# Second chunk of a fused attention and feed-forward kernel: V's copies and low halves ahead of a row tile and a row of outputs

## The chip, the cores and the metric

The kernel runs on one core of one Trainium2 chip. The metric is the device time of one execution in microseconds (us). The engines are called as in the profile: PE is TensorE, DVE is VectorE, ACT is ScalarE, POOL is GpSimd, SP is SyncE, which here only issues DMAs. Each engine runs its own queue of instructions in order and waits on semaphores that the others raise.

## What is computed

The input is 4096 rows of 512 numbers (2 x 2048 x 512). Each row goes through a latent attention block and a feed-forward block with ternary weights, each behind a layer norm and with a layer norm on its result before the residual is added. Cut to what matters:

```
h  = layernorm(x)
Q, V = h @ Wq.T + bq, h @ Wv.T + bv             # 16 heads of 32
logits = Q . latent_keys / sqrt(32)             # 64 latents per head
w, idx = top_k(logits, 4);  p = softmax(w)
attn = (sum_k p_k * latent[idx_k] + V) @ Wo.T + bo
x  = x + layernorm(attn)
g  = layernorm(x)
u, gt = g @ ternary(W_up).T, g @ ternary(W_gate).T   # 2048 wide
x  = x + layernorm((silu(u) * gt) @ ternary(W_down).T)
```

Every matrix product works on float16 pairs: a float32 operand is split in a high half (a copy to float16) and a low half (what the copy left over), and both are multiplied.

## The kernel before

The rows are cut into eight chunks of 512, each of four row tiles of 128. The code of one chunk is a `body(i, kind, att, ffn, nxt)` that every engine has for itself: `"first"`, `"second"`, then a loop of `"mid"` bodies, `"last"` and `"tail"`. A body of chunk i holds the attention of chunk i, the feed-forward of chunk i-1, and the first layer norm of chunk i+1, interleaved. The order on each engine is the order of the calls in its body. `late` is true in the second body alone; there the ternary weights are still being made.

At the end of the second body stands the seam that the change touches. The row of work on each engine is:

- **PE** (from the call `v(0)` on): V of two banks (`v(0)`, `v(1)`), the down products of row tiles 0 and 1 (`down`, L692), `v(2)`, `v(3)` (L539), the weighted latents added to V's accumulators (`weigh`, L631), `down(2)`, then the output projection `wo(0)` to `wo(3)` (L651, 12 matmuls each), and `down(3)`. `wo(0)` waits before each of its four groups k for the low half `a_lo` number k+1. The next body begins with Q (`q`, L539 with wq), which needs the next chunk's four transposed row tiles (XT), and with `upgate(0, half)` and `upgate(1, half)` (L673), of which half 0 needs the first two transposed tiles of X1T and half 1 the last two.
- **ACT**: `f_rows(t)` (L980) scales row tile t of the down product into the output buffer; `s1_rows(1, t)` normalises row tile t of the next chunk (L787, tile xn) and makes its high half (L800, tile halves); `vw(m)` copies V's accumulator m out of its bank (L943, tile p32, shown as p) and makes its high half (L948, qaT_hi). xn is one buffer, so `s1_rows` of tile t waits for the low half of tile t-1. p32 has two buffers, so `vw(2)` and `vw(3)` wait for the low halves 0 and 1. The high half of row tile 2 waits until the transpose of tile 0 has read its buffer.
- **POOL**: `s1_lo(1, t)` makes the row tile's low half (L1233), `f_out(t)` adds the residual to the output buffer (L1221) and releases the store, `low_a(m)` makes the low halves of V (L1186, qaT_lo), `rstd_f` and `rstd_y` compute reciprocal deviations (L1146).
- **DVE**: `f_a(t)`, `f_b(t)` make statistics and factors of a down row (rcf L1554, nbf L1560), `y_a(t)` takes an output projection out of its bank (L1599) with its statistics, `y_b`, `y_c` make the residual sum and the second layer norm's factors (x L1619, nbx L1633), `t2_lo` its low half (L1472), `f_row(3)` the last output row (L1588). `f_b(2)` stands ahead of `y_a(1)`.
- **SP**: store 0, reload 0, store 1, reload 1 of the residual (L431, L440; both of t wait for `f_out(t)`), then the four transposes XT (L371), then reload 2 and store 2, then the four transposes X1T (L371).

Of the kernel before, what the change touches and what calls it, by code (L numbers as in the profile page):

```python
# [80 lines left out]
def build(nc, x, Wq, Wv, Wo, small, bo, Wu, Wg, Wd, out):  # L81
    NCH = x.shape[0] * x.shape[1] // CH
    with ExitStack() as ctx:
# [148 lines left out]
        def wait(eng, s, c, per, n):  # L232


            v = c * per + max(n, 0)
            if not isinstance(v, int) or v > 0:
                eng.wait_ge(s, v)


        def wait_p(eng, c, tiles):  # L240

            for s in range(2):
                wait(eng, p_t[s], c, 32, 16 * ((tiles + 1 - s) // 2))
# [52 lines left out]
        def residual(is_last):  # L296

            return x_in if is_last else x1

        def split_buffers(kind, c, t):  # L300


            if kind == "first" and c == 0:
                return (qaT[t // 2][:, :, :].rearrange("p k t -> p (k t)").bitcast(F32)[:, (t % 2) * D:(t % 2 + 1) * D],
                        PT[:, 0, 2 * t:2 * t + 2, :].rearrange("p k t -> p (k t)"))
            if kind == "first":
                return Lb[:, t % 2, 0:D // NL, 0:NL], out_buf[t % 2].bitcast(F16)
            return xn[:, :], halves[:, t % 2, :]
# [7 lines left out]
        def wide(v, rows):  # L316

            return v.rearrange("p (a l) -> p a l", l=NL) if len(rows.shape) == 3 else v
# [13 lines left out]
        def down_bank(kind, t):  # L332

            if kind == "last" and t >= 2:
                return ring[:, plans["last"][("WO", 0, t - 2)][0], :]
            return ug[:, t, :]
# [429 lines left out]
        def _(act):  # L766
            def body(i, kind, att, ffn, nxt):
# [3 lines left out]
                def s1_rows(c, t):  # L771

                    wait(act, ln1_bias, i + c, 1, 1)

                    if kind == "first" and c == 0:
                        pass
                    elif kind == "first" and t < 2:

                        wait(act, p_ready, i, TT, 3 + t)
                    elif kind == "first":  # L780
                        wait(act, x_lo, i + c, TT, t - 1)
                    elif t:
                        wait(act, x_lo, i + c, TT, t)
                    else:
                        wait(act, x1_lo, i - 1, TT, TT)
                    rows, half = split_buffers(kind, c, t)
                    act.activation(rows, wide(x_in[:, t, :], rows), ACT.Identity, scale=rs1[:, t:t + 1],  # L787
                                   bias=nb1[:, t:t + 1]).then_inc(xn1_ready, 1)
                    wait(act, xn1_ready, i + c, TT, t + 1)

                    if kind == "first" and c == 0:
                        pass
                    elif kind == "first" and t < 2:

                        wait(act, p_raw, i, TT, TT)
                    elif t < 2:
                        wait_p(act, i + c, 0)
                    else:
                        wait(act, x_t[t % 2], i + c - 1, 32, 16)
                    act.activation(wide(half[:, 0:D], rows), rows, ACT.Copy).then_inc(x_hi, 1)  # L800
# [136 lines left out]
                def vw(m):  # L937
                    wait(act, vw_done, i, KD, m + 1)
                    if m < 2:
                        wait(act, q_lo, i, KD, KD)  # L940
                    else:
                        wait(act, a_lo, i, KD, m - 1)
                    act.activation(p32[:, m % 2, :], ring[:, plan[("VW", 0, m)][0], :], ACT.Identity,  # L943
                                   scale=PROJ, bias=bvs[:, m:m + 1]).then_inc(a32_ready, 1)
                    wait(act, a32_ready, i, KD, m + 1)

                    wait(act, l_done, i, 8, 8)
                    act.activation(qaT[0][:, m, :], p32[:, m % 2, :], ACT.Copy).then_inc(a_hi, 1)  # L948
# [26 lines left out]
                def f_rows(t):  # L975

                    wait(act, f_bias, j, TT, t + 1)

                    wait(act, out_stored[(t + 2) % 4], j, 16, 16 if t >= 2 else 0)
                    act.activation(out_buf[t % 2], down_bank(kind, t), ACT.Identity, scale=rcf[:, t % 2:t % 2 + 1],  # L980
                                   bias=nbf[:, t % 2:t % 2 + 1]).then_inc(f_sum, 1)
# [83 lines left out]
                late = kind == "second"  # L1065
# [42 lines left out]
                    f_rows(0)  # L1108
                if nxt:
                    s1_rows(1, 0)  # L1110
                    s1_rows(1, 1)
                    f_rows(1)
                if att:
                    for m in range(KD):
                        vw(m)
                if nxt:
                    s1_rows(1, 2)
                    s1_rows(1, 3)
                    f_rows(2)
                elif att:  # L1120
                    f_rows(1)
# [6 lines left out]
                if kind == "last":  # L1128
                    f_rows(2)
                    f_rows(3)  # L1130

            bodies(act, body)


        @block.gpsimd
        def _(pool):
# [19 lines left out]
            def body(i, kind, att, ffn, nxt):  # L1156
# [27 lines left out]
                def low_a(m):  # L1184
                    wait(pool, a_hi, i, KD, m + 1)
                    pool.tensor_tensor(qaT[1][:, m, :], p32[:, m % 2, :], qaT[0][:, m, :], ALU.subtract).then_inc(a_lo, 1)  # L1186
# [31 lines left out]
                def f_out(t):  # L1218

                    wait(pool, f_sum, j, TT, t + 1)  # L1220
                    pool.tensor_tensor(out_buf[t % 2], out_buf[t % 2], residual(kind == "tail")[:, t, :],  # L1221
                                       ALU.add).then_inc(out_ready, 1)
# [7 lines left out]
                def s1_lo(c, t):  # L1230
                    wait(pool, x_hi, i + c, TT, t + 1)
                    rows, half = split_buffers(kind, c, t)
                    pool.tensor_tensor(wide(half[:, D:2 * D], rows), rows, wide(half[:, 0:D], rows), ALU.subtract).then_inc(x_lo, 1)  # L1233

                def rstd_f(t):
                    rstd(rsf[:, t % 2:t % 2 + 1], vaf[:, t % 2:t % 2 + 1], 1, f_var, j, TT, t + 1, f_rstd)
# [43 lines left out]
                late = kind == "second"  # L1280
# [30 lines left out]
                if nxt:  # L1311
                    rstd_f(1)
                    s1_lo(1, 0)
                    s1_lo(1, 1)
                    f_out(1)
                if att:
                    for m in range(KD):
                        low_a(m)
                if nxt:
                    s1_lo(1, 2)  # L1320
                    s1_lo(1, 3)
                    rstd_f(2)
                elif ffn:
                    rstd_f(1)
                    f_out(1)
# [19 lines left out]
                elif ffn:  # L1345
                    f_out(3)

            bodies(pool, body)


# [511 lines left out]
```

## Time and profile before

| what | us |
|---|---|
| median of 3 runs | 1040.43 (1039.85 to 1041.40) |
| the profiled execution, its device time | 1039.87 |
| its span in the trace | 1038.0 |
| PE busy | 967.7 (93%) |
| DVE, POOL, ACT busy | 733.5, 542.9, 514.2 |

The mean granted TensorE clock of the profiled execution is 0.979 of full speed. The profiled execution has 1.9 us outside its span. The second body's seam lies between 186 and 246 us of the span; the first waits for transposed tiles of the chunk after it end at 245 us, and from there on PE shows no wait for another engine until 330 us. Times below are us from the start of the span.

### The profile page before, as it was taken

The numbers are of one execution on the slowest core, as the hardware profiler recorded it, in microseconds if no ns is written. First come the engines' busy times: TensorE is split into PE (matmuls) and PEld (weight loads), VectorE is DVE, ScalarE is ACT, GpSimd is POOL, SyncE is SP. The second block draws the span as 40 slices with busy tenths as digits, with TensorE's granted clock in tenths as the row PEclk, the third lists the DMA queues.
The fourth block names the chain that finished last, engine by engine and source line by source line (L and its number), as shares of the span: only waits on it lengthen the run. The fifth ranks groups of instructions, "written<-read, shape, count | busy, mean of one in ns | idle before, by whom it ended". The sixth has DMA issues, their size and how long they took to land.

```text
span 1038.0 us, 17906 instructions
## 1 busy us (share of the span) xinstructions
PE 967.7 (93%) x5738; PEld 470.3 (45%) x5738; DVE 733.5 (71%) x2664; ACT 514.2 (50%) x803; POOL 542.9 (52%) x452
## 2 busy tenths in 40 slices
PE   3374999999999999999999999999999999999997
PEld 2331544345444454445444454445444454445443
DVE  7986899556993779845994768936896669845433
ACT  4867886345444455245444445344553454423430
POOL 2476356654665546564565445654465546643330
PEclk9786999999999999999999999999999999999999
DMA  8935503433123311233023331244022321212001
GB/s 261 399 97 90 164 1 82 100 88 98 22 31 93 84 58 31 53 99 92 11 39 84 77 82 21 41 103 110 10 41 61 91 42 21 41 41 62 1 1 41
DMA packets 149330, 76.91 MB, mean 74 GB/s; under 512 B 135824, under 2 KB 135824, under 8 KB 148112
## 3 DMA queue, kind: packets, MB, share of 16 engines
q1 hardware_dynamic: 149264, 76.18, 29.3%
q8 instruction: 23, 0.38, 0.2%
q14 instruction: 43, 0.35, 0.1%
HBM read 34.21 MB, written 8.39 MB: 41 GB/s over the span
## 4 chain that ended last, share of the span: by engine, by line
PE 60%; DVE 17%; ACT 7%; issue 6%; POOL 6%; DMA 4%; SPq 0%; DVEq 0%; ACTq 0%; POOLq 0%
PE ug L673 34%; PE ug L692 12%; PE ring L539 8%; PE ring L651 4%; DVE Lr L1514 2%; PE ring L587 2%; POOL halves L1233 1%; DVE halves L1472 1%; DVE ugt L1477 1%; DVE v L1492 1%; DMA X1T<-halves 1%; DVE stx L1622 1%; DVE row L1599 1%; DVE x L1619 1%; DVE sty L1602 1%
## 5 line engine op out<-in xcount | busy, mean ns | idle before, releaser
L1210 POOL TENSOR_TENSOR hT<-ugt,hT 128x512 f16<-128x512 f32 x128 | 166.9, 1304 | 164.6 <-ACT hT L973 164.6
L673 PE MATMUL ug<-X1T,TU 128*128 128x512 f16 (+1 forms) x1152 | 245.1, 356 | 6.4 <-DVE ugt L1482 4.6
L673 PE MATMUL ug<-X1T,TG 128*128 128x512 f16 (+1 forms) x1152 | 244.9, 355 | 0.0
L692 PE MATMUL ug<-TD,hT 128*128 128x512 f16 x960 | 212.7, 381 | 2.4 <-ACT TD L854 2.4
L960 ACT ACTIVATE ugt<-ug,cu 128x512 f32<-128x512 f32 x128 | 87.9, 687 | 202.8 <-PE ug L673 202.0
L673 PEld LDWEIGHTS ug<-X1T,TU 128*128 128x128 f16 x1152 | 109.9, 98 | 116.8 <-DVE ugt L1482 5.6
L673 PEld LDWEIGHTS ug<-X1T,TG 128*128 128x128 f16 x1152 | 112.7, 98 | 108.7
L1477 DVE SCALAR_TENSOR_TENSOR ugt<-ugt,ug 128x512 f32<-128x512 f32 x128 | 87.2, 681 | 99.2 <-ACT ugt L960 98.0
L692 PEld LDWEIGHTS ug<-TD,hT 128*128 128x128 f16 x960 | 93.6, 98 | 118.8 <-issue 5.3
L1514 DVE MATCH_REPLACE8 Lr<-v,Lb 128x68 f32<-128x68 f32 x512 | 102.3, 211 | 0.0
L1541 DVE BATCH_NORM_STATS2 stf<-ug 128x6 f32<-128x512 f32 x30 | 20.8, 694 | 99.4 <-PE ug L692 99.4
L1482 DVE SCALAR_TENSOR_TENSOR ugt<-ugt,ug 128x512 f32<-128x512 f32 x128 | 87.9, 687 | 4.4
L539 PE MATMUL ring<-XT,wq_hi 128*128 128x512 f16 (+1 forms) x288 | 79.2, 362 | 7.6 <-DVE wq_lo L1450 5.8
L1192 POOL TENSOR_TENSOR Lb<-Lb,v 128x1024 f32<-128x1024 f32 x32 | 63.2, 1976 | 37.9 <-DVE Lr L1514 37.9
L973 ACT ACTIVATE hT<-ugt 128x512 f16<-128x512 f32 x128 | 79.6, 622 | 3.1 <-DVE ugt L1482 3.1
L1492 DVE MAX8 v<-Lb 128x8 f32<-128x64 f32 x512 | 69.0, 208 | 0.4
L539 PE MATMUL ring<-XT,wv_hi 128*128 128x512 f16 x224 | 66.6, 379 | 0.0
L1204 POOL TENSOR_TENSOR p<-Lb,r 128x1024 f32<-128x1024 f32 x24 | 45.6, 1900 | 34.8 <-DVE Lb L1529 34.8
L651 PE MATMUL ring<-wo_hi,qaT_hi 128*128 128x512 f16 x128 | 50.4, 394 | 2.9 <-POOL qaT_lo L1177 2.0
L935 ACT ACTIVATE halves<-p 128x1024 f16<-128x1024 f32 x29 | 30.4, 1048 | 45.7 <-POOL p L1204 41.2
L539 PE MATMUL ring<-XT,wq_lo 128*128 128x512 f16 (+1 forms) x144 | 52.1, 362 | 0.0
L814 ACT ACTIVATE xn<-x,nbx,rsx 128x512 f32<-128x512 f32 x28 | 22.7, 810 | 57.4 <-DVE nbx L1633 38.5
(195 smaller groups left out, 1479.2 us busy)
## 6 DMA issues: line engine op xcount, KB each, us to landing
out_dram<-Lr SPq DMA_DIRECT2D x32, 256.0 KB, 3.2
x_in<-in_x SPq DMA_DIRECT2D x7, 1024.0 KB, 5.5
x<-in_x SPq DMA_DIRECT2D x28, 256.0 KB, 3.3
PT<-in_Wd SPq DMA_DIRECT2D x8, 512.0 KB, 6.9
hT<-in_Wu SPq DMA_DIRECT2D x4, 512.0 KB, 9.4
hT<-in_Wg SPq DMA_DIRECT2D x4, 512.0 KB, 15.0
x_in<-in_Wd SPq DMA_DIRECT2D x4, 512.0 KB, 4.8
x_in<-in_x SPq DMA_DIRECT2D x4, 256.0 KB, 4.5
```

The lines of the kernel that those rows point to most:

```text
L539: last = pe.matmul(bank[:, cols], wT[w][a][:, k, m * P:(m + 1) * P], XT[:, b, k, cols], start=(n == 1), stop=(stop and n == 3 * KD), skip_ ...
L651: last = pe.matmul(ring[:, bank, :], qaT[a][:, k, t * P:(t + 1) * P], wT[2][b][:, k, :], start=(n == 1), stop=(n == 3 * KD))
L673: last = pe.matmul(ug[:, 2 * (e % 2) + s, cols], w[:, k, e * P:(e + 1) * P], X1T[:, b, k, cols], start=(k == 0 and b == 0), stop=(k == KD ...
L692: last = pe.matmul(down_bank(kind, t), hT[:, a, e, t * P:(t + 1) * P], td[:, e, :], start=(first and e == of[0] and a == 0), stop=(final a ...
L960: act.activation(ugt[:, e % 2, :], ug[:, 2 * (e % 2), :], ACT.Tanh, scale=cu[:, 0:1]).then_inc(tanh_ready, 1)
L973: act.activation(hT[:, 0, e, :], ugt[:, 2 + e % 2, :], ACT.Copy).then_inc(h_hi, 1)
L1192: pool.tensor_tensor(buf, buf, v8[:, t % 2, :, 0:1].broadcast_to([P, H, NL]), ALU.subtract).then_inc(shifted, 1)
L1210: pool.tensor_tensor(hT[:, 1, e, :], ugt[:, 2 + e % 2, :], hT[:, 0, e, :], ALU.subtract).then_inc(h_lo, 1)
L1477: dve.scalar_tensor_tensor(out=ugt[:, e % 2, :], in0=ugt[:, e % 2, :], scalar=1.0, in1=ug[:, 2 * (e % 2), :], op0=ALU.add, op1=ALU.mult).t ...
L1482: dve.scalar_tensor_tensor(out=ugt[:, 2 + e % 2, :], in0=ugt[:, e % 2, :], scalar=HS, in1=ug[:, 2 * (e % 2) + 1, :], op0=ALU.mult, op1=ALU ...
L1492: last = dve.max(v8[:, t % 2, h, :], Lb[:, t % 2, h, 0:NL])
L1514: last = dve.match_replace(Lr[:, h, :], v8[:, t % 2, h, :], Lb[:, t % 2, h, :], HIT)
```

## The change

In the second body alone, two calls on ACT and two on POOL go behind four others. On ACT, `s1_rows(1, 1)` and `f_rows(1)` stood ahead of the four `vw`; now the four `vw` come first, then `f_rows(1)`, then `s1_rows(1, 1)`. On POOL, `s1_lo(1, 1)` and `f_out(1)` stood ahead of the four `low_a`; now the four `low_a` come first, then `f_out(1)`, then `s1_lo(1, 1)`. No instruction is added or taken away, and the orders on PE, DVE and SP are the same.

```
@@ ACT @@
                     f_rows(0)
                 if nxt:
                     s1_rows(1, 0)
-                    s1_rows(1, 1)
-                    f_rows(1)
+                    if not late:
+                        s1_rows(1, 1)
+                        f_rows(1)
                 if att:
                     for m in range(KD):
                         vw(m)
                 if nxt:
+                    if late:
+                        f_rows(1)
+                        s1_rows(1, 1)
                     s1_rows(1, 2)
@@ POOL @@
                 if nxt:
                     rstd_f(1)
                     s1_lo(1, 0)
-                    s1_lo(1, 1)
-                    f_out(1)
+                    if not late:
+                        s1_lo(1, 1)
+                        f_out(1)
                 if att:
                     for m in range(KD):
                         low_a(m)
                 if nxt:
+                    if late:
+                        f_out(1)
+                        s1_lo(1, 1)
                     s1_lo(1, 2)
```

POOL's queue at the end of the second body, before, from `f_out(0)` on (x4 and x2 are instructions in a row that read alike; the brackets name the semaphores waited for, f_sum comes from `f_rows`, x_hi from `s1_rows`, a_hi from `vw`):

```order
69 L1221 TENSOR_TENSOR Lr<-Lr,x1 128x512 [waits f_sum]
70 L1146 TENSOR_TENSOR rsf<-vaf,nh 128x1 [waits f_var]
71 L1233 TENSOR_TENSOR halves<-xn,halves 128x512 [waits x_hi] x2
72 L1221 TENSOR_TENSOR Lr<-Lr,x1 128x512 [waits f_sum]
73 L1186 TENSOR_TENSOR qaT_lo<-p32,qaT_hi 128x512 [waits a_hi] x4
74 L1233 TENSOR_TENSOR halves<-xn,halves 128x512 [waits x_hi] x2
75 L1146 TENSOR_TENSOR rsf<-vaf,nh 128x1 [waits f_var]
76 L1146 TENSOR_TENSOR rsy<-vay,nh 128x1 [waits y_var]
```

The same place of POOL's queue after the change (line numbers are four higher there):

```order
69 L1225 TENSOR_TENSOR Lr<-Lr,x1 128x512 [waits f_sum]
70 L1150 TENSOR_TENSOR rsf<-vaf,nh 128x1 [waits f_var]
71 L1237 TENSOR_TENSOR halves<-xn,halves 128x512 [waits x_hi]
72 L1190 TENSOR_TENSOR qaT_lo<-p32,qaT_hi 128x512 [waits a_hi] x4
73 L1225 TENSOR_TENSOR Lr<-Lr,x1 128x512 [waits f_sum]
74 L1237 TENSOR_TENSOR halves<-xn,halves 128x512 [waits x_hi] x3
75 L1150 TENSOR_TENSOR rsf<-vaf,nh 128x1 [waits f_var]
76 L1150 TENSOR_TENSOR rsy<-vay,nh 128x1 [waits y_var]
```

The four low halves moved ahead of `f_out(1)` and of one row tile; the three row tiles that are left now stand in one piece.

ACT's queue at the same place, before, from `s1_rows(1, 0)` on (vw_done comes from PE's `weigh`, a_lo and x_lo from POOL):

```order
191 L787 ACTIVATE xn<-x_in,nb1,rs1 128x512 [waits x1_lo,ln1_bias]
192 L800 ACTIVATE halves<-xn 128x512 [waits p_t1,p_t0,xn1_ready]
193 L787 ACTIVATE xn<-x_in,nb1,rs1 128x512 [waits x_lo,ln1_bias]
194 L800 ACTIVATE halves<-xn 128x512 [waits p_t1,p_t0,xn1_ready]
195 L980 ACTIVATE Lr<-ug,nbf,rcf 128x512 [waits f_bias]
196 L943 ACTIVATE p32<-ring,bvs 128x512 [waits q_lo,vw_done]
197 L948 ACTIVATE qaT_hi<-p32 128x512 [waits l_done,a32_ready]
```

And after the change:

```order
192 L800 ACTIVATE halves<-xn 128x512 [waits p_t1,p_t0,xn1_ready]
193 L943 ACTIVATE p32<-ring,bvs 128x512 [waits q_lo,vw_done]
194 L948 ACTIVATE qaT_hi<-p32 128x512 [waits l_done,a32_ready]
...
199 L943 ACTIVATE p32<-ring,bvs 128x512 [waits a_lo,vw_done]
200 L948 ACTIVATE qaT_hi<-p32 128x512 [waits l_done,a32_ready]
201 L980 ACTIVATE Lr<-ug,nbf,rcf 128x512 [waits f_bias]
202 L787 ACTIVATE xn<-x_in,nb1,rs1 128x512 [waits x_lo,ln1_bias]
```

The eight instructions of `vw` moved ahead of three: the two of row tile 1 and the row of the second down product.

## Rows read from the trace of the kernel before

**Rows 1.** The chain that ended last: shares of the span by engine.

```profile
PE 60%; DVE 17%; ACT 7%; issue 6%; POOL 6%; DMA 4%; SPq 0%; DVEq 0%; ACTq 0%; POOLq 0%
```

**Rows 2.** Timeline of PE: start, length (us), instruction, idle before and its releaser.

```profile
189.83 9.63 PE L692 MATMUL ug<-TD,hT 128*128 128x512 f16 x36 [1.86 <-ACT TD L854]
...
204.56 0.63 PE L631 MATMUL ring<-PT,latV_hi 64*32 64x512 f16 x16
...
212.91 0.38 PE L651 MATMUL ring<-wo_hi,qaT_hi 128*128 128x512 f16 x1
...
215.69 0.39 PE L651 MATMUL ring<-wo_hi,qaT_hi 128*128 128x512 f16 x1 [0.42 <-POOL qaT_lo L1186]
...
224.12 7.07 PE L692 MATMUL ug<-TD,hT 128*128 128x512 f16 x32
231.03 0.59 PE L539 MATMUL ring<-XT,wq_hi 128*128 128x512 f16 x2
...
243.13 1.04 PE L673 MATMUL ug<-X1T,TU 128*128 128x256 f16 x8
...
245.35 1.03 PE L673 MATMUL ug<-X1T,TU 128*128 128x256 f16 x8 [0.30 <-DMA X1T<-halves]
```

**Rows 3.** Timeline of ACT, same columns.

```profile
204.05 0.63 ACT L800 ACTIVATE halves<-xn 128x512 f16<-128x512 f32 x1
206.66 0.81 ACT L787 ACTIVATE xn<-x_in,nb,rs 128x512 f32<-128x512 f32 x1 [1.99 <-POOL halves L1233]
...
208.71 0.68 ACT L943 ACTIVATE p<-ring,bvs 128x512 f32<-128x512 f32 x1
...
215.49 0.63 ACT L800 ACTIVATE halves<-xn 128x512 f16<-128x512 f32 x1 [0.38 <-DMA XT<-halves]
217.45 0.81 ACT L787 ACTIVATE xn<-x_in,nb,rs 128x512 f32<-128x512 f32 x1 [1.33 <-POOL halves L1233]
```

**Rows 4.** Timeline of POOL.

```profile
205.13 1.16 POOL L1233 TENSOR_TENSOR halves<-xn,halves 128x512 f16<-128x512 f32 x1
...
209.33 1.27 POOL L1221 TENSOR_TENSOR Lr<-Lr,x 128x512 f32<-128x512 f32 x1
...
213.24 2.39 POOL L1186 TENSOR_TENSOR qaT_lo<-p,qaT_hi 128x512 f16<-128x512 f32 x2 [0.40 <-ACT qaT_hi L948]
...
219.00 1.16 POOL L1233 TENSOR_TENSOR halves<-xn,halves 128x512 f16<-128x512 f32 x1 [1.65 <-ACT halves L800]
220.12 0.55 POOL L1146 TENSOR_TENSOR rsf<-vaf,nh 128x1 f32<-128x1 f32 x1
```

**Rows 5.** Timeline of DVE.

```profile
220.70 0.16 DVE L1554 TENSOR_TENSOR rcf<-rsf,cf 128x1 f32<-128x1 f32 x1 [2.15 <-POOL rsf L1146]
...
221.03 0.74 DVE L1599 SCALAR_TENSOR_TENSOR row<-ring,clo,bo_b 128x512 f32<-128x512 f32 x1
...
239.58 0.74 DVE L1588 SCALAR_TENSOR_TENSOR Lr<-ug,rcf,x_kept 128x512 f32<-128x512 f32 x1
```

**Rows 6.** The chain in order of time, cut to two transposes: start, length, what.

```profile
211.65 3.76 DMA XT<-halves
...
242.16 3.05 DMA X1T<-halves
```

**Rows 7.** Timeline of the last chunk: weigh on PE, V's copies on ACT, low halves on POOL.

```profile
917.01 0.62 PE L631 MATMUL ring<-PT,latV_hi 64*32 64x512 f16 x16
...
917.92 0.69 ACT L943 ACTIVATE p<-ring,bvs 128x512 f32<-128x512 f32 x1 [6.25 <-PE ring L631]
...
922.02 2.40 POOL L1186 TENSOR_TENSOR qaT_lo<-p,qaT_hi 128x512 f16<-128x512 f32 x2 [0.28 <-ACT qaT_hi L948]
```

**Rows 8.** PE by stretches: us, PE busy (instructions), granted clock, DMA share, GB/s.

```profile
101.00:102.00 1.00, 0.00 (x0) 1.00 0.27 53
...
190.00:191.00 1.00, 1.00 (x3) 0.50 0.58 66
```

**Rows 9.** Timeline of PE in the first body, before the second chunk's Q.

```profile
102.15 0.59 PE L539 MATMUL ring<-XT,wq_hi 128*128 128x512 f16 x2 [1.67 <-DMA XT<-Lr]
```

More of the change, by code:

```diff
@@ L1110, in body @@
                     s1_rows(1, 0)
-                    s1_rows(1, 1)
-                    f_rows(1)
+                    if not late:
+                        s1_rows(1, 1)
+                        f_rows(1)
                 if att:
@@ L1116, in body @@
                 if nxt:
+                    if late:
+                        f_rows(1)
+                        s1_rows(1, 1)
                     s1_rows(1, 2)
@@ L1313, in body @@
                     s1_lo(1, 0)
-                    s1_lo(1, 1)
-                    f_out(1)
+                    if not late:
+                        s1_lo(1, 1)
+                        f_out(1)
                 if att:
@@ L1319, in body @@
                 if nxt:
+                    if late:
+                        f_out(1)
+                        s1_lo(1, 1)
                     s1_lo(1, 2)
```

## The prediction, written before the changed kernel was run

> **What bounds the kernel now.** I read first the chain that ended last. PE holds 60% of it and DVE 17% [rows 1], so PE sets the end in most places and something else in a few, and the question is what sets it at this seam. PE's timeline shows three waits there. Before the third group of `down` PE waits 1.86 us for the ternary weights [rows 2]; the change comes later than that. In `wo(0)` it waits for the low halves of V, the row that starts at 215.69 [rows 2]. And at 245.35 the first matmul of `upgate(0, 1)` waits for the last transpose X1T [rows 2, 6].
>
> The third wait is the important one. From 245.35 on PE runs without waiting, so whatever moves that instant moves the end. What moves it is not PE's own pace but a second path, which the timelines give step by step: `f_out(1)` on POOL, 209.33 to 210.60 [rows 4]; store 1 and reload 1 on SP; the transpose XT of tile 0 from 211.65, landed 3.76 later at 215.41 [rows 6]; the high half of tile 2 on ACT, which waits for that landing [rows 3]; its low half on POOL; tile 3 on ACT at 217.45, which waits for POOL [rows 3]; its low half on POOL from 219.00 and behind it `rstd_f(2)` at 220.12 [rows 4]; `f_b(2)` on DVE at 220.70, which had waited 2.15 us for it, and behind it `y_a(1)` at 221.03 [rows 5]. From there DVE is busy with `y_a`, `y_b`, `y_c` and `t2_lo` in a row, down to the transpose X1T from 242.16, landed 3.05 later at 245.21 [rows 6].
>
> **What the change takes away: the wait in `wo(0)`.** The 48 matmuls of `wo` take from 212.91 to 224.12, 11.21 us. At the pace of `down(3)`, 32 in 231.03 - 224.12 = 6.91 us or 0.216 each [rows 2], they would take 10.37. So 0.84 us is lost, all of it ahead of groups 3 and 4 of `wo(0)`. When will the low halves be ready after the change? The last chunk shows the same instructions with nothing ahead of them: `vw(0)` starts 917.92 - 917.01 = 0.91 us after `weigh(0)`, and the fourth low half ends at 922.02 + 2.40 = 924.42, which is 6.50 us after `vw(0)` starts [rows 7]. Here `weigh(0)` starts at 204.56 [rows 2], so `vw(0)` starts at 205.47; ACT is free from 204.68 on [rows 3] and POOL from 206.29 [rows 4], before the first low half could start anyway. The fourth low half ends at 205.47 + 6.50 = 211.97 instead of 213.24 + 2.39 = 215.63 [rows 4]. PE reaches `wo(0)` at 212.91, so the wait goes entirely: **-0.84 us for PE**, if nothing else bound it.
>
> **What it delays: `f_out(1)`, and with it the second path.** On POOL `f_out(1)` now stands behind the four low halves, so it starts at 211.97 instead of 209.33: 2.64 later, say 2.6, since neighbours on POOL overlap by 0.04. (On ACT, `f_rows(1)` comes behind `vw(3)` and ends half a us before that; it does not decide.) SP issues its DMAs in order and has `f_out(1)` in front of all four transposes, so transpose 0 goes from 211.65 to 214.25. The rest of the path follows step by step with nothing to absorb it. Row tile 1 costs nothing of its own: its low half follows `f_out(1)` on POOL and ends at 214.4, and transpose 1 is not due before 213.07 + 2.6. ACT's tile 2 waits for transpose 0's landing, now at 218.0, tile 3 for POOL behind that, `rstd_f(2)` for tile 3's low half, DVE for `rstd_f(2)`. DVE has waited 2.15 us there already and will wait longer; `y_a(1)` starts at 223.6. Between it and the last X1T DVE has no idle stretch over 0.5 us, so I take no slack out of it. The last X1T lands at 247.8 and PE starts `upgate(0, 1)` at 245.35 + 2.6 = 247.95. That `wo` is done 0.84 earlier is worth nothing, since it only makes PE wait longer. **+2.6 us on the path that sets the end.**
>
> The bounds of this term. If the clock had not been low from 190 on (below), `weigh(0)` would start up to 1.7 us earlier, but POOL is only free at 206.29 [rows 4] and needs twice 2.40 us for the four low halves [rows 7] plus a gap of 0.1 to 0.3 between them; `f_out(1)` would start at about 211.2, +1.9. So the term lies between 1.9 and 2.6. What else is delayed has room: the last XT lands near 226.5, and Q wants it at 231.03 - 0.84 = 230.2 [rows 2]. The second X1T lands at about 240.0, half a us before `upgate(0, 0)` wants it. `f_row(3)` ends at 240.32 + 2.6 = 242.9 [rows 5], and `upgate(1, 0)` waits for it from 243.13 - 0.84 = 242.3 on [rows 2]: 0.6 us that vanishes in the longer wait behind it.
>
> **What PE's longer idle costs.** `upgate(1, 0)` takes two steps of 0.87, from 243.0 to 244.8, and then PE has nothing to do until 247.95: 3.1 us, after 0.6 us just before. In the trace of before, an idle time of 1.86 us ending at 189.83 [rows 2], with one of 0.5 us shortly ahead of it, is followed by the granted clock at 0.50, the lower level of 1.2 GHz [rows 8]. It cost 1.7 us: 36 matmuls took 9.63, where at full clock they take 36 x 0.216 + 0.16 = 7.94 [rows 2]. Against that, an idle time of 1.67 us ending at 102.15 [rows 9] left the clock at 1.00 [rows 8]. The new idle time is nearly twice the longer of the two, so I take the fall as the likelier: **+1.7 us**. PE is the bound from there on, so all of it counts. The bounds are 0 and 3.4 (a fall that lasts twice as long). [...]
>
> **The sum.** -0.84 is hidden; 2.6 + 1.7 = +4.3 us. On the profiled execution of before that is 1039.87 + 4.3 = 1044.2, on the median 1040.43 + 4.3 = 1044.7. Not every execution need have the full term at both places, so I forecast between the two: **1044.4 us**, range of this case alone 1043.4 to 1045.2.
>
> **The rivals.**
>
> (B) The clock stays at full speed after the idle time. For it: the row that did not fall after 1.67 us [rows 8, 9]. Against it: 3.1 us is well above both rows. Then only the path counts: +1.9 to +2.6, so 1042.3 to 1043.0.
>
> (C) The second path has slack that I do not see, and the gain in `wo(0)` stays: not slower, but faster. One mechanism would do it: SP's transposes would have to be waiting for something other than `f_out(1)`, such as PE's last read of XT by `v(3)`, and DVE likewise at `f_b(2)`. It decides if the transposes start less than 0.4 us later than before. The time would be 1040.43 - 0.84 + (0 to 0.3) = 1039.6 to 1039.9. Against it: store 1 starts within 0.05 us of `f_out(1)`'s end and the transpose follows the two DMAs at once, and `v(3)` is over by 204.56 [rows 2]. I give it little.
>
> (D) The clock falls and stays low twice as long, because Q's successor begins with short matmuls and an interrupted stretch. +2.6 + 3.4 = +6.0, so 1046.4.
>
> (E) The change has its waits elsewhere, and absorbs part of the delay on DVE: `y_a(0)` comes 0.84 earlier. But DVE idles between `y_a(0)` and `f_b(2)`, so this moves nothing; what is left is a delay of about 1 us without a fall of the clock, 1041.0 to 1041.8.
>
> **How the numbers follow.** Forecast 56%, B 28%, C 4%, D 6%, E 6%. The range goes from 1042.0, which takes in B whole, to 1046.0, which leaves out most of D, C and E: 1042.0 to 1046.0 holds about 84% by this count, and I keep it, as the terms are known to no better than some tenths. A measurement of this kernel can tell about 0.2% or 2.1 us from no change, that is 1038.3 to 1042.5. Slower by more: the forecast, D, and some three quarters of B, 0.83. Within: the low part of B, E and C, 0.15. Faster by more than 0.2% has no mechanism here, since the wait removed is 0.84: 0.02.
>
> **What the profile of the changed kernel would show.** Right: no wait in `wo(0)`, whose 48 matmuls take 10.4 us; `vw(0)` at about 205.5; `f_out(1)` at 212.0; the first XT issued at 214.2; `rstd_f(2)` at 222.7; `y_a(1)` at 223.6; a PE wait for X1T of about 3 us ending near 247.9; and a granted clock of 0.5 just before or after that. Wrong: an X1T that lands before 246.5 (the path has slack), or a wait for X1T of 3 us with the clock at 1.00 throughout, which is B. A time below 1041 would mean that the second path is not what sets the end.

## The result, and the profile after

The changed kernel takes 1044.76 us, the median of 6 runs from 1043.57 to 1045.15. The kernel before, with six runs by now, takes 1040.15 (1039.59 to 1041.40). The ratio is 1.0039, with a 95% interval of 1.0028 to 1.0049, which is 2.9 to 5.1 us; by the medians it is 4.6 us slower. The forecast was 1044.4 with a range of 1042.0 to 1046.0. The profiled execution of after has a span of 1043.1 us against 1038.0.

This is PE's timeline of the changed kernel over the same stretch; the rows answer to [rows 2]:

```profile
190.25 9.60 PE L692 MATMUL ug<-TD,hT 128*128 128x512 f16 x36 [1.86 <-ACT TD L854]
...
204.96 0.63 PE L631 MATMUL ring<-PT,latV_hi 64*32 64x512 f16 x16
...
213.30 0.38 PE L651 MATMUL ring<-wo_hi,qaT_hi 128*128 128x512 f16 x1
...
223.66 7.07 PE L692 MATMUL ug<-TD,hT 128*128 128x512 f16 x32
...
243.83 1.05 PE L673 MATMUL ug<-X1T,TU 128*128 128x256 f16 x8 [0.80 <-DVE Lr L1596]
...
248.79 1.87 PE L673 MATMUL ug<-X1T,TU 128*128 128x256 f16 x8 [3.04 <-DMA X1T<-halves]
```

The 48 matmuls of `wo` now take 223.66 - 213.30 = 10.36 us, where they took 11.21: the 0.84 us that the change was good for have been taken. In their place stand a new wait of 0.80 us for `f_row(3)`, and one of 3.04 us for the last X1T, which was 0.30 before. To compare the two traces, take off what this execution was already late before the seam: the third group of down matmuls starts at 190.25 against 189.83, 0.42 us.

POOL and ACT of the changed kernel (they answer to [rows 3, 4]):

```profile
207.29 2.40 POOL L1190 TENSOR_TENSOR qaT_lo<-p,qaT_hi 128x512 f16<-128x512 f32 x2 [0.59 <-ACT qaT_hi L948]
209.97 2.40 POOL L1190 TENSOR_TENSOR qaT_lo<-p,qaT_hi 128x512 f16<-128x512 f32 x2 [0.28 <-ACT qaT_hi L948]
212.32 1.27 POOL L1225 TENSOR_TENSOR Lr<-Lr,x 128x512 f32<-128x512 f32 x1
213.55 1.16 POOL L1237 TENSOR_TENSOR halves<-xn,halves 128x512 f16<-128x512 f32 x1
219.63 1.16 POOL L1237 TENSOR_TENSOR halves<-xn,halves 128x512 f16<-128x512 f32 x1 [4.93 <-ACT halves L800]
222.43 1.15 POOL L1237 TENSOR_TENSOR halves<-xn,halves 128x512 f16<-128x512 f32 x1 [1.65 <-ACT halves L800]
223.54 0.55 POOL L1150 TENSOR_TENSOR rsf<-vaf,nh 128x1 f32<-128x1 f32 x1
```

```profile
205.87 0.69 ACT L943 ACTIVATE p<-ring,bvs 128x512 f32<-128x512 f32 x1 [0.78 <-PE ring L631]
...
218.93 0.63 ACT L800 ACTIVATE halves<-xn 128x512 f16<-128x512 f32 x1 [3.31 <-DMA XT<-halves]
```

DVE, and the chain in order of time, of the changed kernel (they answer to [rows 5, 6]). DVE waits 6.03 us for `rstd_f(2)` where it waited 2.15:

```profile
224.13 0.16 DVE L1562 TENSOR_TENSOR rcf<-rsf,cf 128x1 f32<-128x1 f32 x1 [6.03 <-POOL rsf L1150]
...
224.46 0.74 DVE L1607 SCALAR_TENSOR_TENSOR row<-ring,clo,bo_b 128x512 f32<-128x512 f32 x1
```

```profile
214.63 4.21 DMA XT<-halves
...
245.60 3.05 DMA X1T<-halves
248.79 5.04 PE ug L673 x32
```

The chain contains the whole second path: V's copies and low halves, `f_out(1)`, the transpose XT, the two row tiles, DVE's row of work (with a last piece on ACT), the transpose X1T. Its last row above shows the price of the clock: the 32 matmuls of `upgate(0, 1)` and `upgate(1, 1)` take 5.04 us, where before the same chain has them at 3.65. The granted clock (stretch, PE busy, clock, DMA share, GB/s) says why. It is at 0.50, the level of 1.2 GHz, from a little before PE resumes:

```profile
247.00:248.00 1.00, 0.00 (x0) 1.00 1.12 210
248.00:249.00 1.00, 0.21 (x2) 0.63 1.31 342
249.00:250.00 1.00, 1.00 (x6) 0.50 0.55 147
250.00:251.00 1.00, 1.00 (x7) 0.50 0.97 295
251.00:252.00 1.00, 1.00 (x8) 0.67 1.04 442
252.00:253.00 1.00, 1.00 (x11) 1.00 0.24 98
```

So the 5.1 us between the two spans are 0.42 us of lateness before the seam, 2.57 us by which `f_out(1)` starts later (212.32 - 0.42 - 209.33), 0.45 us by which the first XT takes longer to land (4.21 against 3.76), 1.39 us of the lower clock, and 0.3 us behind the seam, most of it in one later wait for X1T (0.70 us at 488.8, where it was 0.46).

### The profile page after: what moved, and what is told of

Its sections match the earlier page's. It is cut to its first block, busy times and chain, and to the rows that moved or that the text cites. A ratio compares the mean times of both kernels' runs of the same rounds, so it can differ in the third digit from the quotient of the medians.

```text
span 1043.1 us, 17906 instructions
## 1 busy us (share of the span) xinstructions
PE 968.3 (93%) x5738; PEld 471.0 (45%) x5738; DVE 733.8 (70%) x2664; ACT 514.1 (49%) x803; POOL 543.6 (52%) x452
## 4 chain that ended last, share of the span: by engine, by line
PE 61%; DVE 16%; ACT 7%; issue 6%; POOL 6%; DMA 3%; SPq 0%; DVEq 0%; ACTq 0%; POOLq 0%
PE ug L673 34%; PE ug L692 13%; PE ring L539 8%; PE ring L651 4%; DVE Lr L1522 2%; PE ring L587 2%; DVE ugt L1485 1%; POOL halves L1237 1%; POOL qaT_lo L1190 1%; DVE v L1500 1%; DMA X1T<-halves 1%; DVE stx L1630 1%; DVE halves L1480 1%; DVE x L1627 1%; DVE row L1607 1%
```

## Experiments

Each was timed beside the kernel before on the same chip (one chip for the first eight, another for the last two), and each ratio is taken against those runs. The kernel before had a median of 1039.73 (23 runs) beside the first four, 1040.48 (27 runs) beside the next four and 1040.53 (23 runs) beside the last two.

The traces of these kernels can also be compared over the seam alone, whatever came before or after it: from the start of the third group of down matmuls to the start of the first matmul of 512 columns of `upgate(2)`. The kernel before takes 60.55 us for it and the changed kernel 64.96. These are single executions.

**Which half of the change costs?** The change moves two things behind V's copies: row tile 1, and the second down row with `f_out(1)`. One kernel moves the row tile alone. Cut from ACT, and the same on POOL with `s1_lo` and `f_out`:

```
                     s1_rows(1, 0)
-                    s1_rows(1, 1)
+                    if not late:
+                        s1_rows(1, 1)
                     f_rows(1)
                 if att:
                     for m in range(KD):
                         vw(m)
                 if nxt:
+                    if late:
+                        s1_rows(1, 1)
```

> Half of the change: row tile 1 (on ACT and POOL) goes behind V's copies and low halves, the second down row stays ahead of them. Theory (the store row f_out(1) holds back SP's transposes, and the path through them sets the end): f_out(1) ends at about 209, transpose 0 goes at once, transpose 1 at about 215 and tile 3's low half ends where it did before. The wait in wo(0) is gone but hidden. Time 1040.2, between 1039.7 and 1041.0. Rival (row tile 1's own lateness is what costs, since tiles 2 and 3 queue behind it): the time stays near the changed kernel's, 1043.5 to 1045.

Measured: 1040.23 (12 runs), ratio 1.0005 (0.9996 to 1.0015). The theory holds. POOL's timeline of this kernel, whose seam begins 1.18 us later than that of before (third down group at 191.01):

```profile
208.57 1.27 POOL L1224 TENSOR_TENSOR Lr<-Lr,x 128x512 f32<-128x512 f32 x1 [1.16 <-ACT Lr L980]
209.81 2.39 POOL L1189 TENSOR_TENSOR qaT_lo<-p,qaT_hi 128x512 f16<-128x512 f32 x2
212.49 2.40 POOL L1189 TENSOR_TENSOR qaT_lo<-p,qaT_hi 128x512 f16<-128x512 f32 x2 [0.28 <-ACT qaT_hi L948]
215.09 1.16 POOL L1236 TENSOR_TENSOR halves<-xn,halves 128x512 f16<-128x512 f32 x1 [0.21 <-ACT halves L800]
...
220.69 1.15 POOL L1236 TENSOR_TENSOR halves<-xn,halves 128x512 f16<-128x512 f32 x1 [1.65 <-ACT halves L800]
```

Row tile 1's low half starts at 215.09, 5.7 us later than in the kernel before by its own start, and yet tile 3's starts at 220.69, 0.5 us later than before once the 1.18 is off. A row tile behind V's copies costs next to nothing, because in the kernel before the tiles behind it had been waiting for the transpose anyway. One part of the expectation was missed: PE still waits in `wo(0)`. In this execution the clock stayed up behind 190 (more on that below), so PE reached `wo(0)` sooner.

```profile
214.94 0.39 PE L651 MATMUL ring<-wo_hi,qaT_hi 128*128 128x512 f16 x1 [0.42 <-POOL qaT_lo L1189]
```

The other kernel moves the down row alone and leaves the row tile ahead:

```
                     s1_rows(1, 0)
-                    s1_rows(1, 1)
-                    f_rows(1)
+                    s1_rows(1, 1)
+                    if not late:
+                        f_rows(1)
                 if att:
                     for m in range(KD):
                         vw(m)
                 if nxt:
+                    if late:
+                        f_rows(1)
```

> The other half: the second down row goes behind V's copies and low halves, row tile 1 stays ahead. Theory: the copies start 2.7 us later than in the changed kernel, f_out(1) and the transposes with them, so the last X1T and the end come 2.7 us later than there: 1047.4, between 1046.5 and 1048.5. Rival (row tile 1's lateness costs): it is on time here, so 1040 to 1041.

Measured: 1046.34 (5 runs from 1045.91 to 1046.60), ratio 1.0062 (1.0049 to 1.0075). This is the half that costs, and by itself it costs more than the whole change. It is 1.6 us above the changed kernel rather than 2.7, just below the expected range. I had counted the copies as starting 2.7 us later. `f_out(1)` starts at 214.30, 2.0 us later than in the changed kernel (2.3 with both starts of the seam counted), and the first XT lands 3.80 us after its issue instead of 4.21, so the last X1T is used 1.8 us later than in the changed kernel. PE now waits three times, and the clock falls twice:

```profile
242.67 1.04 PE L673 MATMUL ug<-X1T,TU 128*128 128x256 f16 x8 [2.41 <-DMA X1T<-halves]
...
245.39 1.89 PE L673 MATMUL ug<-X1T,TU 128*128 128x256 f16 x8 [0.24 <-DVE Lr L1594]
...
250.34 1.55 PE L673 MATMUL ug<-X1T,TU 128*128 128x256 f16 x8 [2.12 <-DMA X1T<-halves]
```

```profile
244.00:245.00 1.00, 1.00 (x6) 0.50 0.00 0
...
248.00:249.00 1.00, 0.22 (x2) 1.00 0.68 135
...
251.00:252.00 1.00, 1.00 (x7) 0.50 0.83 262
```

The first of these falls does not add its whole price: PE was going to wait for X1T again at 250.

**Is it the order on SP?** The changed kernel, with the first transpose taken out from behind `f_out(1)`:

```
                     for t in range(2):
                         out(t)
                         if nxt:
                             reload(t)
+                        if kind == "second" and t == 0:
+                            s1(0)
                 if nxt:
-                    for t in range(TT):
+                    for t in range(1 if kind == "second" else 0, TT):
                         s1(t)
```

> The changed kernel, with one more move on SP in the second body: the transpose of row tile 0 ahead of store 1 and reload 1, so that it no longer waits for f_out(1). Theory: the high half of tile 2 no longer waits for its landing, tile 3's low half ends 2.7 us earlier than in the changed kernel, the time falls back to 1040.5 (1040.0 to 1041.2; up to 1.4 more if an idle time of some 1.6 us still lowers the clock). Rival (POOL's three row tiles in one piece are the cause, whatever SP does): 1043.5 to 1045.

Measured: 1040.51 (11 runs), ratio 1.0002 (0.9993 to 1.0012). With one DMA moved, the changed kernel is back at the time of the kernel before. SP's timeline shows the transpose going 6 us before store 1:

```profile
205.56 0.65 SPq L440 DMA_DIRECT2D x<-in_x  x1
206.86 1.23 SPq L371 DMA_TRANSPOSE XT<-halves  x1
212.98 0.34 SPq L431 DMA_DIRECT2D out_dram<-Lr  x1
```

`f_out(1)` itself is nearly as late here as in the changed kernel. It starts 21.42 us after the third down group, where the kernel before has 19.50 and the changed kernel 22.07 (the clock stayed up behind 190 here too, so V's copies came sooner; the 1.92 us are the prediction's lower bound of 1.9 for this case). The last X1T is used 55.57 us after the third down group, against 55.52 before and 58.54 in the changed kernel. What costs is therefore not that the output row comes late, but that SP keeps the first transpose behind it. PE's timeline has a surprise:

```profile
245.84 1.03 PE L675 MATMUL ug<-X1T,TU 128*128 128x256 f16 x8 [2.89 <-DMA X1T<-halves]
```

PE waited 2.89 us, and the clock was at 1.00 all the same in every microsecond from 243 to 252. PE waited that long because it came early, with no wait in `wo(0)` and the full clock behind 190:

```profile
245.00:246.00 1.00, 0.16 (x2) 1.00 1.05 318
246.00:247.00 1.00, 1.00 (x11) 1.00 0.58 131
```

I come back to this below.

**Does DVE pass the delay on?** The changed kernel, with `y_a(1)` put into the time in which DVE waits for `rstd_f(2)`:

```
                 if att:
                     y_a(0)
+                    if late:
+                        y_a(1)
                 if nxt:
                     f_b(2)
                 if att:
-                    y_a(1)
+                    if not late:
+                        y_a(1)
                     y_b(0)
```

> The changed kernel, with one more move on DVE in the second body: y_a(1) ahead of f_b(2), so that DVE uses the time in which it waits for rstd_f(2). Theory (DVE's row of work behind f_b(2) passes every delay on to the last X1T): the last X1T lands 1.9 us earlier than in the changed kernel; 1042.9 if the clock still falls, 1041.5 if the shorter idle time of 2.0 us leaves it up. Rival (DVE is not on the path): 1044 to 1045, as the changed kernel.

Measured: 1043.01 (5 runs from 1042.42 to 1044.93), ratio 1.0038 (1.0025 to 1.0051). The median is the one expected with the fall of the clock, and the clock does fall in its profile (0.50 from 248 to 250). But the interval overlaps with that of the changed kernel, so this run alone does not tell the theory from its rival. The trace says more: X1T is used at 246.79, with the third down group at 189.49, so 57.30 us after it, where in the changed kernel it is 58.54. The move saves 1.2 us of the path, not 1.9. That DVE passes the delay on is shown by this trace and not by the times.

**Both moves, with and without the change.**

> The changed kernel with both moves, transpose 0 ahead of store 1 on SP and y_a(1) ahead of f_b(2) on DVE, in the second body. Theory: the last X1T lands before PE wants it, so the 0.84 us that the change takes out of wo(0) and the 0.47 us that PE waited for X1T before it both count: 1.3 under the kernel before, 1038.9 (1038.3 to 1039.6). Rival (something else sets the end at this seam): 1040 or more.

> The kernel before, with the same two moves on SP and DVE and without the change. Theory: only the 0.47 us wait for X1T goes, the wait in wo(0) stays: 1039.7 (1039.2 to 1040.3), 0.8 above the kernel with the change and both moves. Rival (the moves on SP and DVE alone bring the whole gain): the same time as that kernel.

Measured: 1039.57 with the change (11 runs), ratio 0.9991 (0.9982 to 1.0000); 1040.07 without it (11 runs), ratio 0.9996 (0.9987 to 1.0005). The signs and the order are the expected ones. With the second path shortened the change is no longer a loss, and the medians differ by 0.5 us of the 0.8 forecast; but the two intervals overlap, so that the saved wait in `wo(0)` now counts is likely and not shown by these times. The two traces show a part of it: the seam takes 59.59 us with the change and 59.91 without, 0.3 us apart. With the change X1T still comes too late for PE, which waits 0.20 us for it:

```profile
245.38 1.03 PE L675 MATMUL ug<-X1T,TU 128*128 128x256 f16 x8 [0.20 <-DMA X1T<-halves]
```

**What does the lower clock cost?** To take the idle time away without the wait, the first pass of the middle loop was written out, and 12 spare matmuls were put where PE waits. The loop alone first, as control:

```
+            body(2, "mid", True, True, True)
-            with eng.Fori(2, NCH - 1) as i:
+            with eng.Fori(3, NCH - 1) as i:
```

> Control: the changed kernel with the first pass of the loop over the middle chunks written out ahead of the loop, the same work in the same order. Expected 1044.7 (1044.0 to 1045.4), as the changed kernel, with the clock at 0.50 after the wait for X1T.

Measured: 1045.00 (5 runs), ratio 1.0048 (1.0034 to 1.0061). It behaves like the changed kernel: X1T waited for 3.04 us, clock at 0.50 behind it. Then, in that pass, ahead of `upgate(0, 1)`:

```
                 for half in range(2):
+                    if kind == "mid" and isinstance(i, int) and half == 1:
+                        wait(pe, q32_ready, i, KD, 1)
+                        for n in range(12):
+                            pe.matmul(ring[:, plan["Q", 0, 0][0], :], wT[0][0][:, 0, 0:P], XT[:, 0, 0, :],
+                                      start=True, stop=True)
                     upgate(0, half)
```

> The control with 12 spare matmuls of 512 columns into a free bank (their result is not used), 2.6 us of PE work where PE waits for the last X1T. Theory (about 1.4 us of the loss is the lower clock after that idle time): the clock stays at 1.00 through the first products of the third chunk, X1T lands as late as in the control, and the time is 1.4 us under the control, 1043.3 (1042.7 to 1043.8). Rival (the clock costs nothing there): the control's time or more.

Measured: 1042.29 (11 runs), ratio 1.0013 (1.0004 to 1.0022). More work for PE makes the kernel faster by 2.7 us, and the ranges do not overlap (1040.75 to 1042.99 against 1044.51 to 1046.62). That is below the expected range of 1042.7 to 1043.8: 1.4 us were expected. In the two traces the seam itself gives the expected part of that. Control first, then filled:

```profile
249.17 1.87 PE L674 MATMUL ug<-X1T,TU 128*128 128x256 f16 x8 [3.04 <-DMA X1T<-halves]
...
255.63 1.90 PE L674 MATMUL ug<-X1T,TU 128*128 128x512 f16 x8
```

```profile
248.40 1.03 PE L674 MATMUL ug<-X1T,TU 128*128 128x256 f16 x8 [0.45 <-DMA X1T<-halves]
...
253.43 1.90 PE L674 MATMUL ug<-X1T,TU 128*128 128x512 f16 x8
```

From the landing of X1T to the first full matmul of `upgate(2)` the control takes 6.46 us and the filled kernel 5.03: 1.43 us, at clocks of 0.50 and 1.00. X1T is used 58.6 and 58.5 us after the third down group, so the path is as long in both. That the lower clock costs 1.4 us here is shown. The other 1.3 us of the difference between the medians are not explained by it. In the profiled pair, PE's waits for X1T at the later seams come to 2.3 us in the control and 0.6 in the filled kernel; whether the spare matmuls have any part in that stays open, since nothing behind the seam differs. All that follows the seam takes between 786.4 and 788.4 us in the twelve traces of this document, so two single executions can differ by as much without a cause in the kernel.

**Can the waits for X1T at the later seams be had, and the free half of the change with them?** Before, PE waits 1.5 us for X1T behind the seam in three places. One kernel has the move on DVE in the second and all middle bodies and nothing else (`if nxt:` where the piece above has `if late:`); the other adds the half of the change that costs nothing.

> The kernel before (no change), with one move on DVE in the second and in every middle body: y_a(1) ahead of f_b(2). Theory: the path through DVE is a little late at the later seams too (PE waits 1.5 us for X1T there in all, 0.3 us at the second body's seam), so those waits go: 1.8 under the kernel before, and the wait in wo(0) stays. Rival (the waits for X1T are run to run noise of the transposes and would stay): no difference.

Measured: 1039.74 (11 runs), ratio 0.9997 (0.9988 to 1.0005). No difference that can be told, so the expectation of 1.8 us missed. The waits say what went wrong: at the second body's seam PE no longer waits for X1T, and the seam is 0.4 us shorter (60.19). Of the later waits, two of 0.5 and one of 0.6 us in the kernel before, one of 0.5 and the one of 0.6 are still there. The one of 0.6 is at the seam before the tail, where the move does not apply; I had not looked where the three were.

> The same move on DVE in the second and in every middle body, with the half of the change that costs nothing: in the second body row tile 1 behind V's copies and low halves, the second down row ahead of them. Theory: the wait in wo(0) goes as well and now counts, since nothing else is late: 0.8 under the kernel with the move on DVE alone, 2.6 under the kernel before. Rival (the wait in wo(0) is hidden by another one): the same as with the move on DVE alone.

Measured: 1039.23 (12 runs), ratio 0.9990 (0.9982 to 0.9999). This is the lowest median of all, 1.3 us under the kernel before where 2.6 were forecast. Its interval just leaves out 1, as one of ten intervals, and overlaps with that of the DVE move alone, 0.5 us above it. So it is probably better than the kernel before, by a tenth of a percent, and half of what I forecast. The trace shows that "nothing else is late" did not hold. The seam takes 59.86 us, 0.3 less than with the DVE move alone; the clock stayed up behind 190, PE still waits 0.40 us in `wo(0)`, and then again for X1T:

```profile
245.66 1.03 PE L673 MATMUL ug<-X1T,TU 128*128 128x256 f16 x8 [1.58 <-DMA X1T<-halves]
```

## Why the prediction was right

The forecast was slower by 4.3 us, made of +2.6 for the second path, +1.7 for the clock and 0.84 that hides. Measured is 4.6. Step by step, with the 0.42 us by which this execution came late to the seam added to the forecast times:

- `vw(0)` at 205.89 forecast, 205.87 measured. The copies and low halves of the last chunk [rows 7] were the right measure for this seam.
- `f_out(1)` at 212.39, measured 212.32. The first XT issued at 214.67, measured 214.63.
- `y_a(1)` at 224.0, measured 224.46; the last X1T used at 248.37, measured 248.79. Both are 0.4 to 0.5 late, and all of it is the landing of the first XT, 4.21 us instead of 3.76 [rows 6]. I had carried the old duration over and given it no range. The rigid part from `y_a(1)` on passed the delay on without slack: 24.33 us from `y_a(1)` to the use of X1T, and 24.32 before. The prediction called it DVE's row of work down to the transpose. In the chain of before its last piece runs through ACT, from the factors of tile 2 to `t2_lo` of tile 3, and DVE has one idle stretch of 0.52 us in it where the prediction says none over 0.5. Neither changed the sum:

```profile
236.40 0.82 ACT xn L814
...
240.61 1.40 DVE halves L1472
```

- `upgate(1, 0)` waited 0.80 us for `f_row(3)`, forecast 0.6, hidden as said.
- The clock fell, and cost 1.39 us where I had 1.7. The term was taken from a place where the clock fell when PE had just resumed, at 189.83 (granted clock 0.97 in the microsecond from 189 on, 0.50 behind it [rows 2, 8]). Here it had fallen before PE resumed at 248.79 (0.63 in the microsecond from 248 on), so part of the time at the lower level passed idle. Four other traces bear this out. From the use of X1T to the first matmul of 512 columns it takes 5.03 us at full clock. In the two kernels where the clock fell only after PE had resumed (the down row behind, `y_a(1)` ahead) it takes 6.70, 1.67 more; in the other two, where it fell during the wait (the row tile behind, the loop written out), 6.50 and 6.46.

The errors, +0.45 and -0.3, nearly cancel. That the sum came out closer than its terms is luck. The forecast of 1044.4 also lay below the sum on the median (1044.7), on the argument that not every execution has the full terms; the six runs, with 1044.76 as their median, give no sign of that.

The rivals: B (the clock stays up) gave 1042.3 to 1043.0, and none of the six runs lies there. The experiments show that it was a real case: with 2.89 us of waiting in the kernel with the early transpose the clock stayed at 1.00. C (slack in the second path) fell with the two halves of the change, and E's slack on DVE is not there either: `y_a(0)` came 0.9 us earlier (216.09 - 0.42, against 216.55), and DVE only waited longer behind it.

What I had not seen is how the clock before the seam plays in. In the profile of before it is at 0.50 from 190 to 193, and I treated the 1.7 us there as given. In four of the twelve traces it stayed up behind the same wait (both halves of the change, the early transpose, and the row tile behind with the DVE move), and the same 36 matmuls took 7.94 us. This is the kernel with the row tile behind:

```profile
191.01 7.94 PE L692 MATMUL ug<-TD,hT 128*128 128x512 f16 x36 [1.86 <-ACT TD L854]
...
247.04 1.87 PE L673 MATMUL ug<-X1T,TU 128*128 128x256 f16 x8 [2.75 <-DMA X1T<-halves]
```

PE then came to `wo(0)` 1.7 us earlier and gained nothing by it, since the second path sets the end there. It lost 0.6 us again in `wo(0)` and waited 2.75 us for X1T, where it would have been 1.7 with the lower clock behind 190 (an estimate: 2.75 less the 1.1 us that were left of the 1.7), and this time the clock fell there:

```profile
247.00:248.00 1.00, 0.96 (x5) 0.50 1.09 133
```

That execution took 1042.73, 2.5 above its kernel's median of 1040.23. About 1.5 of that is the lower clock (6.50 against 5.03 us), and it came to the seam 1.2 us later than the trace of before. So a time won by PE ahead of a place where it waits for another path can even be lost twice. It need not be: in the kernel with the early transpose the clock stayed up at both places. It would also explain why the runs of the kernel before reach from 1038.2 to 1043.2, but there is no trace of its longer executions here, so that is argued and not shown.

## What to carry to other kernels

When two pieces of work swap places on an engine, list what each releases in the other queues. Here the order of SP's queue tied a transpose of the next chunk to a store of the last one, and moving 0.8 us of waiting off PE put 2.6 us on the path that the transpose begins. Before taking a wait from an engine, look for the next wait of the same engine for another path: if there is one before the end, the gain only makes that wait longer, and on PE a wait of about 3 us can bring a lower clock on top (four of the five such waits in these traces did). Moving one DMA issue in front of an unrelated one can be the whole cure, as it was here (1044.76 to 1040.51).

## What the runs showed of the hardware

The granted clock is not a function of the length of one idle time. It fell after a PE wait of 1.86 us with 0.5 us shortly before it in eight of the twelve traces ([rows 2, 8] for the kernel before), and did not after the same two waits in the other four. It fell with waits of 2.75, 3.03, 3.04 and 3.04 us (in four of these kernels), and of 2.41 and 2.12 us in the kernel with the down row behind; it did not after 2.89 us in the kernel with the early transpose, nor after 1.58 us in the last one. The same wait of the same code can thus go either way. The Trainium skill says of the slow matmuls at the start of a kernel that their number is "run-variable" (TensorE: Matmul & The Clock Gate, Part 1: The HAM clock gate). These traces show that falls in the middle of a kernel vary as well, eight against four at one place. The price of a fall at this seam was 1.4 to 1.7 us. With 12 spare matmuls in the idle time the clock stayed up in the one execution profiled, and all 11 runs were faster than all 5 of the control.

The transposes of one row tile on this path took between 3.0 and 4.5 us from issue to landing (3.05 for the last X1T, 4.47 for an XT in the kernel with the early transpose). The one that lies on this path took 3.76 us in one trace and 4.21 in the other, behind the same two DMAs; such a difference is a tenth of what the whole change moved, and no range of mine had it. Why it differs is open.
